# Cross-attention block on one core: scores before the next key, and a weight's upper parts moved from GpSimd to ScalarE in the opening

## The reference

```python
q  = layernorm(x) * q_norm_g + q_norm_b
kv = layernorm(ctx) * kv_norm_g + kv_norm_b
qp, kp, vp = q @ Wq.T + bq, kv @ Wk.T + bk, kv @ Wv.T + bv
scores = qh @ kh.T / sqrt(32) - spatial_scale[h] * dist(query_xy, token_xy) + spatial_offset[h]
scores = where(token_mask, scores, -inf)
x = x + softmax(scores) @ vh @ Wo.T + bo
x = x + gelu(layernorm(x) @ W1.T + b1) @ W2.T + b2
```

## Time and profile before

| | |
|---|---|
| median of 3 runs | 1207.32 us (1204.98 to 1208.12) |
| the profiled execution, own time | 1204.9 us |
| its span, the first to the last instruction | 1203.0 us |
| TensorE busy | 98% of the span |
| VectorE, ScalarE, GpSimd busy | 76%, 72%, 79% |
| mean granted TensorE clock | 0.997 |

### The profile page before, as it was taken

One profiled execution on the slowest core, in us unless ns is written; L12 is line 12 of the kernel. 1 busy time (PEld: TensorE's weight loads), 2 busy tenths in 40 slices (PEclk: granted clock), 3 DMA queues, 4 the chain that ended last, 5 costly groups with the idle time before them and its releaser, 6 DMA issues.

```text
span 1203.0 us, 27763 instructions
## 1 busy us (share of the span) xinstructions
PE 1181.3 (98%) x9632; PEld 806.3 (67%) x9632; DVE 912.4 (76%) x2482; ACT 863.4 (72%) x1964; POOL 953.5 (79%) x1198
## 2 busy tenths in 40 slices
PE   7899999999999999999999999999999999999999
PEld 4566666666676766667676666667666666766666
DVE  7987768787787978877797888778787877668322
ACT  5798787858677786867778786877778587757232
POOL 6889989788897988789798878889887887758321
PEclk9999999999999999999999999999999999999999
DMA  9776768989799898979989998889989797978553
GB/s 264 202 190 182 183 181 184 208 190 234 164 232 200 186 215 191 217 180 229 189 189 226 188 217 168 212 203 217 216 181 217 188 218 160 187 169 173 148 152 103
DMA packets 434524, 233.22 MB, mean 194 GB/s; under 512 B 349888, under 2 KB 374864, under 8 KB 434384
## 3 DMA queue, kind: packets, MB, share of 16 engines
q1 hardware_dynamic: 434384, 231.45, 83.7%
HBM read 109.66 MB, written 12.58 MB: 102 GB/s over the span
## 4 chain that ended last, share of the span: by engine, by line
PE 90%; ACT 4%; DVE 3%; DMA 1%; issue 1%; SPq 1%; DVEq 0%; ACTq 0%
PE ps_up L920 26%; PE ps_down L940 26%; PE ps_qk L821 13%; PE ps_vo L843 6%; PE ps_s L864 4%; PE ps_pv L846 3%; PE ps_pv L905 3%; PE ps_vo L846 3%; ACT soft L1111 1%; PE ps_down L968 1%; DVE soft L1441 1%; PE ps_down L876 1%; DMA w<-x_scratch 0%; ACT pT_whole L1124 0%; DMA w_stage<-in_w_qkv 0%
## 5 line engine op out<-in xcount | busy, mean ns | idle before, releaser
L920 PE MATMUL ps_up<-hT,w 128*128 128x256 f16 x3072 | 377.0, 273 | 0.0
L1111 ACT ACTIVATE soft<-soft,neg_max 128x256 f32<-128x256 f32 x512 | 255.6, 500 | 163.1 <-DVE neg_max L1441 161.8
L1441 DVE CUSTOM_DVE_ANT_0 soft<-ps_s,soft,factor 128x256 f32<-128x256 f32 x506 | 223.2, 477 | 188.8 <-PE ps_s L864 188.6
L940 PE MATMUL ps_down<-w,hid 128*128 128x512 f16 x1476 | 359.6, 378 | 0.8 <-ACT pT_whole L1124 0.6
L920 PEld LDWEIGHTS ps_up<-hT,w 128*128 128x128 f16 x3072 | 300.6, 98 | 85.9
L1683 POOL TENSOR_SCALAR p_nat<-soft,row_inv 128x256 f16<-128x256 f32 x448 | 265.9, 604 | 71.5 <-DVE row_inv L1454 67.8
L1692 POOL TENSOR_SCALAR soft<-dist,scale_neg,offset 128x512 f32<-128x512 f32 x256 | 271.4, 1060 | 17.3 <-DVE p_nat L1460 15.5
L1460 DVE SCALAR_TENSOR_TENSOR p_nat<-soft,row_inv,p_nat 128x256 f16<-128x256 f32 x448 | 268.5, 639 | 0.8 <-POOL p_nat L1683 0.8
L1164 ACT ACTIVATE u<-ps_up,bias,up_scale 128x256 f32<-128x256 f32 x256 | 142.5, 557 | 126.2 <-PE ps_up L920 123.4
L940 PEld LDWEIGHTS ps_down<-w,hid 128*128 128x128 f16 x1476 | 141.5, 97 | 127.0 <-issue 2.9
L1700 POOL TENSOR_SCALAR hid<-u,hid_scale 128x1024 f16<-128x1024 f32 x63 | 72.9, 1157 | 46.5 <-ACT u L1170 46.5
(11 more groups left out here) (180 smaller groups left out, 1549.2 us busy)
## 6 DMA issues: line engine op xcount, KB each, us to landing
w<-x_scratch SPq DMA_DIRECT2D x252, 256.0 KB, 3.1
stack<-qk_parts SPq DMA_DIRECT2D x256, 96.0 KB
raw<-in_ctx SPq DMA_DIRECT2D x32, 256.0 KB, 3.5
raw<-in_x SPq DMA_DIRECT2D x32, 256.0 KB, 4.2
c_stage<-in_w SPq DMA_DIRECT2D x16, 512.0 KB, 5.0
x<-in_x SPq DMA_DIRECT2D x32, 256.0 KB, 3.5
out<-x SPq DMA_DIRECT2D x31, 256.0 KB, 3.4
tok_rows<-in_tok_xy SPq DMA_DIRECT2D x16, 256.0 KB, 3.6
```

What stands on the lines that cost most here:

```text
L920: mm = e.matmul(ps_up[s % 2][:, 0:L], w_1_sb[:, wp, k, m * P:(m + 1) * P], hT[:, b % 2, :, xp * KT + k, :], start=(k, wp, xp) == (0, 0, 0) ...
L940: mm = e.matmul(ps_down[tt][:], left, w_2_sb[:, s % W2_RING, wp, :], start=first, stop=last)
L1111: e.activation(soft[:, ring, lc, :], soft[:, ring, lc, :], ACT.Exp, scale=-1.0, bias=neg_max[:, ring, lc:lc + 1], accum_out=row_sum[:, rin ...
L1441: e.tensor_tensor_reduce(soft[:, ring, lc, :], score_bank(i)[:, lc * T:(lc + 1) * T], soft[:, ring, lc, :], factor[:, 0:1], 3.0e38, ALU.ad ...
```

## The change

Seven edits:

- **Scores first.** The key of group 1 goes from slot -2 to -1, where it stands behind the scores of item 0. All that follows it moves one slot: its parts to slot 0, the query to 1, its parts to 2, the four copies to 3. The key of group 2 goes from slot 1 to 2, its parts to 3; its query stays. On ScalarE the upper parts of group 1 stand ahead of the slot's exponentials.
- **W_q's upper parts** (all four pieces of the rest) go from GpSimd to ScalarE, in slot -3 behind the square root of the distances.
- **W_q's lower parts:** the first two pieces go from slot -3 to slot 0, behind the maximum of item 0; the last two from slot 0 to 1.
- **W_k's lower parts:** one piece in slot -6 and three in -4, where there were two and two.
- **W_v's norm:** `total` goes from slot -3 to -1 behind the scores of item 0, `square_norm` from -2 to 0 behind the maximum of item 0, `norm_root` from -2 to -1. `gains` stays in slot 0.
- **No negation:** the coordinates stay as they are and the square takes scale=-1.0; `small_negate` is gone.
- The waits for the small inputs move with it.

```diff
-        TOTAL = (-30, -28, -3, 0, 2, 5, 9, 13, 17, 20, 23, 26)
-        NORM = (-27, -24, -2, 1, 3, 6, 10, 14, 18, 21, 24, 27)
+        TOTAL = (-30, -28, -1, 0, 2, 5, 9, 13, 17, 20, 23, 26)
+        NORM = (-27, -24, 0, 1, 3, 6, 10, 14, 18, 21, 24, 27)
...
-        def qk_at(slot, first):
-
-            yield from (G for G in due(slot, first, GROUP, N_HG) if G != 1)
-            if slot == first + GROUP + 1:
-                yield 1
+        QK_OPENING = {(1, 0): -1, (1, 1): 1, (2, 0): 2}
+
+        def qk_at(slot, which, by):
+
+            yield from (G for G in due(slot, QK_PROJ + 2 * which + by, GROUP, N_HG) if (G, which) not in QK_OPENING)
+            yield from (G for (G, of), at_slot in QK_OPENING.items() if (of, at_slot + by) == (which, slot))
...
                 if -1 <= slot < UP:
                     scores(slot + 1)
+                if slot == TOTAL_V:
+                    total(AT[SEC_V])
...
+            def query_hi_rest():
+                gate.wait_ge(s_gs, GAINED_Q)
+                for k in range(KT):
+                    e.activation(w_sec[SEC_Q][:, HI, k, P:D], w_stage[SEC_Q][:, k, P:D], ACT.Copy, scale=gain[:, SEC_Q, k:k + 1]).then_inc(s_rhi_q)
...
-                gate.wait_ge(s_cst, 1)
+                gate.wait_ge(s_small, 3 * DMA)
...
-                    e.activation(dst, tok_rows[:, c, :], ACT.Square, bias=q_neg[:, col:col + 1]).then_inc(s_sq)
+                    e.activation(dst, tok_rows[:, c, :], ACT.Square, scale=-1.0, bias=q_cols[:, col:col + 1]).then_inc(s_sq)
...
-                        if not 0 <= slot < UP:
+                        if G == 1 or not 0 <= slot < UP:
                             qk_hi(G, which)
...
+                if slot == -3:
+                    query_hi_rest()
...
-            def small_negate():
-                gate.wait_ge(s_small, 3 * DMA)
-                e.tensor_scalar(q_neg[:], q_neg[:], -1.0, None, ALU.mult).then_inc(s_cst)
...
                 for i in due(slot, 0, ITEM, N_ITEMS):
                     score_max(i)
+                if slot == NORM_V:
+                    square_norm(AT[SEC_V])
+                    weight_lo_rest(SEC_Q, range(2))
...
-                for sec, pieces, at_slot in ((SEC_K, range(2), -6), (SEC_K, range(2, KT), -4), (SEC_Q, range(2), -3), (SEC_Q, range(2, KT), 0)):
+                for sec, pieces, at_slot in ((SEC_K, range(1), -6), (SEC_K, range(1, KT), -4), (SEC_Q, range(2, KT), 1)):
                     if slot == at_slot:
                         weight_lo_rest(sec, pieces)
...
-            def weight_hi_rest(sec, pieces):
+            def key_hi_rest():
                 gate.wait_ge(s_gs, GAINED_Q)
                 gate.wait_ge(s_wpart[SEC_Q], KT)
-                for k in pieces:
-                    e.tensor_scalar(w_sec[sec][:, HI, k, P:D], w_stage[sec][:, k, P:D], gain[:, sec, k:k + 1], 1.0, ALU.mult, ALU.mult).then_inc(s_rhi)
+                for k in range(KT):
+                    e.tensor_scalar(w_sec[SEC_K][:, HI, k, P:D], w_stage[SEC_K][:, k, P:D], gain[:, SEC_K, k:k + 1], 1.0, ALU.mult, ALU.mult).then_inc(s_rhi_k)
...
+                if slot == NORM_V - 1:
+                    norm_root(AT[SEC_V])
...
-                for sec, pieces, at_slot in ((SEC_K, range(KT), -23), (SEC_Q, range(2), -21), (SEC_Q, range(2, KT), -2)):
-                    if slot == at_slot:
-                        weight_hi_rest(sec, pieces)
+                if slot == -23:
+                    key_hi_rest()
```

More of the change, by code:

```diff
@@ L265, in build_block @@
         s_wpart = {1: sem("s_wpart_k"), 0: sem("s_wpart_q")}
-        s_fhi, s_rhi, s_xhi0, s_head0 = sem("s_fhi"), sem("s_rhi"), sem("s_xhi0"), sem("s_head0")
+        s_rhi_k, s_rhi_q = sem("s_rhi_k"), sem("s_rhi_q")
+        s_fhi, s_xhi0, s_head0 = sem("s_fhi"), sem("s_xhi0"), sem("s_head0")
         s_gram, s_spread, s_top = sem("s_gram"), sem("s_spread"), sem("s_top")
@@ L675, in sync_program @@
                         mask_copy(ring)
-                for G in qk_at(slot, QK_PROJ + 4):
+                for G in qk_at(slot, 1, 2):
                     stack_copies(G)
@@ L995, in tensor_program @@
                 for which in range(2):
-                    for G in qk_at(slot, QK_PROJ + 2 * which):
+                    for G in qk_at(slot, which, 0):
                         for _ in range(STEPS):
@@ L999, in tensor_program @@
                 for w in range(N_W):
-                    if slot == TOTAL[w]:
+                    if slot == TOTAL[w] and w != AT[SEC_V]:
                         total(w)
@@ L1185, in scalar_program @@
                 for which in range(2):
-                    for G in qk_at(slot, QK_PROJ + 2 * which + 1):
-                        if not 0 <= slot < UP:
+                    for G in qk_at(slot, which, 1):
+                        if G == 1 or not 0 <= slot < UP:
                             qk_hi(G, which)
@@ L1196, in scalar_program @@
                 for which in range(2):
-                    for G in qk_at(slot, QK_PROJ + 2 * which + 1):
-                        if 0 <= slot < UP:
+                    for G in qk_at(slot, which, 1):
+                        if G != 1 and 0 <= slot < UP:
                             qk_hi(G, which)
@@ L1364, in weight_lo_rest @@
                 for k in pieces:
-                    gate.wait_ge(s_rhi, KT * AT[sec] + k + 1)
+                    gate.wait_ge(s_rhi_k if sec == SEC_K else s_rhi_q, k + 1)
                     sub = e.scalar_tensor_tensor(out=w_sec[sec][:, LO, k, P:D], in0=w_stage[sec][:, k, P:D], scalar=gain[:, sec, k:k + 1],
@@ L1537, in vector_program @@
                         diagonal(w)
-                    if slot == NORM[w]:
+                    if slot == NORM[w] and w != AT[SEC_V]:
                         square_norm(w)
@@ L1545, in vector_program @@
                     hidden_scales()
-                if slot == -26:
-                    small_negate()
                 if slot == -23:
@@ L1759, in gpsimd_program @@
                         x_hi(1, n)
-                for w in range(AT[SEC_V], N_W):
+                if slot == NORM_V - 1:
+                    norm_root(AT[SEC_V])
+                for w in range(AT[SEC_O], N_W):
                     if slot == NORM[w]:
                         norm_root(w)
-                for sec, pieces, at_slot in ((SEC_K, range(KT), -23), (SEC_Q, range(2), -21), (SEC_Q, range(2, KT), -2)):
-                    if slot == at_slot:
-                        weight_hi_rest(sec, pieces)
+                if slot == -23:
+                    key_hi_rest()
                 if slot == -22:
```

8 lines of the change are left out of this document (5 added, 3 removed).

## The result

| | before | after |
|---|---|---|
| median, taken on the same chip | 1204.59 us (1203.99 to 1208.12) | 1210.49 us (1208.85 to 1211.24) |
| the profiled execution, own time | 1204.9 | 1209.96 |
| its span | 1203.0 | 1208.2 |
| mean granted TensorE clock | 0.997 | 0.994 |

The ratio is 1.0041, with a 95% interval of 1.0029 to 1.0053: about 4.9 us slower. It is not the ratio of the two medians, which lie 5.9 us apart, because the executions of before fall into two groups some 3 us apart. The forecast was 2.1 us slower, read as "no change". The sign of the working was right, its size was less than half of what was measured.

The account below looks back on a forecast made before the run. It took VectorE to bound the opening and TensorE from item 6's scores on. Those scores run 2.1 us late, so 1207.32 + 2.1 = 1209.4 us, read as "no change"; range 1205.5 to 1212.0.

Parts of the forecast that it names:

- What bounds it: TensorE holds the chain from item 6's scores at 48.85 us; a shift there reaches the end nearly whole.
- The copies of group 1: Slot 3: copies take 4.1 us from issue, so item 4's scores start at 42.9 against 39.68, 3.2 late.
- Rival 1: Slot 3: item 4's scores don't wait for the copies; 1.3 us less, 1206.0; chance 0.13.
- The first maximum: Opening: item 0's scores at 26.0, so VectorE's maximum starts at 26.4 instead of 27.73, 1.3 us sooner.
- Rival 4: Opening: W_o's load holds item 0's copy, the maximum stays at 27.73, all behind 1.3 us later, 1210.7; chance 0.08.
- VectorE's list to the end of slot 2: From the first maximum to slot 2's end: 12.4 us against 10.9, ending at 38.8 against 38.65.
- rival 2: Behind the first maximum, W_q's four lower parts meet GpSimd: 2.2 us in all on top, 1211.6; chance 0.12.
- From M3 to item 6: From slot 2's end at 38.8 to item 6's scores at 50.9: 12.1 us, those scores 2.1 late.
- rival 3: Clock falls in the wait ahead of item 4's scores: 1211.1, chance 0.10; old fall vanishes instead: 1207.7, chance 0.05.
- W_q's upper parts on ScalarE: Slot -3: four pieces, about 2.2 us, fit ScalarE's idle time from 23.98; nothing lost.
- The scale in the square: Square of the coordinates: the scale rides in the same instruction, free, 0 us.
- the norm: W_v's norm, moved later: square_norm adds 0.2 us to VectorE's list, the later norm_root on GpSimd costs 0.

Follow-up runs that it names:

- e11: Kernel before with W_q's upper parts on ScalarE in slot -3 and ten filler matmuls in slots -4 and -3: 1203.82 us, ratio 0.9988.
- e2: Changed kernel with group 1 and group 2's key back in their old slots, W_q's last two lower parts in slot 0: 1207.96 us, ratio 1.0026.
- e8: Changed kernel with W_o's load issued behind group 0's copies instead of ahead of them: 1212.54 us, one execution.
- e4: Kernel before with only W_q's upper parts moved from GpSimd to ScalarE in slot -3: 1206.3 us, ratio 1.0001.
- e13: Kernel before with ten filler matmuls (6 in slot -4, 4 in slot -3) and nothing else: 1204.74 us, ratio 0.9996.
- e7: Like e2, with W_v's total, square_norm and root also back in slots -3 and -2: 1206.73 us, ratio 1.0009.
- e1: Changed kernel with 12 filler matmuls ahead of item 0's scores and 9 ahead of group 2's key: 1211.14 us, ratio 1.0044.
- e10: Changed kernel with filler matmuls ahead of the clock's fall, 8 in slot -4, 14 in -2, 9 in 2: 1210.15 us, ratio 1.0033.
- e12: Like e10, with W_1's total ahead of group 2's key and item 4's scores waiting for one copy: 1208.37 us, ratio 1.0024.

## Why the prediction was right or wrong

**What bounds it, and that a shift at item 6 reaches the end:** right. 5.3 at S6, 5.2 in the span.

**The copies of group 1:** right as a bound, and the core of the forecast. 4.15 us from the issue to item 4's scores, 4.1 predicted, though no row gave the 0.4 us in it for the receipt. In the kernels whose key and query of group 2 ran at full clock, M3 to S6 took 12.12 to 12.13 in the new slots, and 10.17 to 10.20 in the old ones (e11's 10.55 has that query at 2.77 us): 1.9 us, as the working had it (12.1 against 10.2). Undoing the slots (e2, with W_q's last two lower parts) gave 0.0015 back, 1.8 us with 1.9 on either side, and 2.2 at S6 in the profile. Rival 1, the gain carried, is refuted.

**The first maximum:** this is the largest term that failed, by 1.7 us. The step said that the copy for item 0 would be there at 26.0, "a little behind the load". "A little behind the load" held: it was read at 27.44, 0.3 us behind the load, as in seven other profiles. What failed is the load's own landing, which the step took over from before: 6.1 us behind its issue there, 25.7, but 7.3 in after, 27.1. Rival 4 had the mechanism, at a chance of 0.08, and e8 shows it. My bounds, 25.3 to 26.41, were too narrow: I had bounded the later end by the time of before, as if a copy issued sooner could not land later. Why the load lands later is open, but the runs narrow it. It took 5.6 to 6.3 us in before, e4, e11 and e13, and 7.2 to 8.3 in the nine profiles with the rest of the change, e7 among them (7.7), which has the slots and the norm of before. So it is none of slots, norm and W_q's upper parts by itself; W_q's first lower parts, W_k's split and the negation with its waits are left, and were not tried. The DMA share in 24 to 31 us doesn't tell the two sets apart: 1.02 in after, but 0.87 in before and in e1, whose load took 7.4.

**VectorE's list to the end of slot 2:** 12.78 against 12.4, and that this is close is luck: two errors nearly cancel. VectorE's busy time from M0 to M3 grew by 1.06 us (10.44 to 11.50) and not by 1.5, mainly as the two parts behind the first maximum took 1.14 us together where 1.49 had stood in before's list; its idle time grew by 0.8, which I had at nothing. W_q's four took 0.606 to 0.609 each, so rival 2, that they meet GpSimd, did not come true (the line's instructions in after, ns least/median/most):

```profile
L1376 DVE SCALAR_TENSOR_TENSOR w_q<-w_stage,gain,w_q x4: 606/607/609, 29.0 to 34.7; 128x384 f16<-128x384 f32 x4
```

The rule of the Trainium skill behind it ("SBUF — State Buffer", section "Who interferes with whom") was hardly put to the test: beside either pair GpSimd made the root of a norm, one number for each partition (29.19 and 34.38, 0.85 us), and its bias tiles began at 30.04 and 35.23, when the pairs were all but done. What I left out is what stands between item 0's and item 1's scores now. I costed VectorE's list and ScalarE's, and not TensorE's. With the key (2.72 at half clock) moved behind the first scores and the gram (1.26) behind it, VectorE waited 1.10 us for the gram. The wait is the half clock's: in e10 the key and the gram ran at full clock, VectorE had no wait there, and M1 came 3.3 us behind M0; in after 4.5, before 2.8.

**From M3 to item 6:** 13.27 against 12.1, short by 1.2. At full clock the 12.1 holds (12.12 in e10), so this is the price of the half clock in slot 3, and it came on a way that I had not listed: the key of group 2 took 2.54 us instead of 1.48, W_1's total stands behind it, VectorE waits 2.05 us for that total, and the key's lower parts come so late that TensorE waits 0.95 for them ahead of the query. The 8.0 us that I gave TensorE from item 4's scores to item 6's held, with these 0.95 on top. TensorE's idle stretch of over 2 us came too, but ahead of that key, which waits 2.46 for the query's lower parts, and only 0.57 of it ahead of item 4's scores. That way is also a second bound at full clock, as e12 shows, which the working did not have: with the copies in time the shift would have been no smaller.

**The clock, rival 3:** it came, and not only where I had put it. I looked for one fall ahead of item 4's scores; there was one there (0.57 in 41 to 45 us) and an earlier one, while TensorE waited for item 0's copy (0.51 in 24 to 31). The Trainium skill, "TensorE: Matmul & The Clock Gate", section "HAM oscillation — how this bites in real kernels", describes just this, matmuls that run slow behind a wait for a DMA; the trace agrees with it by the key's 2.72 us against 1.47. I gave the fall 0.10, by one stretch of the steady part, when the opening has long waits of its own. What it is worth here is not fully shown, since fillers moved it rather than ended it. The rows bound it: the two keys lost 1.25 and 1.07 us, 2.3 in all, and e10, with both keys at full clock and the fall on a query between them, was 0.8 sooner at S6.

**The other parts.** W_q's upper parts on ScalarE: 0, as costed (e4, 1.0001). The scale in the square is free as said: the squares took 0.50 us each before and after. Undoing the slots and the norm together (e7) took the ratio from 1.0041 to 1.0009, 3.9 us with 1.9 on either side. How that splits, 1.8 for the slots (e2) and 2.0 for the norm by the ratios, 2.2 and 0.1 by S6 in the profiles, is not shown, nor what the two lower parts behind the first maximum, W_k's split and the negation cost, since e7 is not clear of before (0.9998 to 1.0019). I had costed the norm at 0.2 on VectorE and 0 on GpSimd and had not asked which TensorE instruction waits for it: in the order of e2 it is W_o's gram, by 0.91 us; in the full change the key stands in that gap.

So the measured 4.9 us against the forecast's 2.1 are three terms at once (1.7, 0.4 and 1.2, together 3.2 at S6 by the profile), and they come from one habit: each engine's list, and the load, was costed by itself, at the durations of before. The forecast of the median itself, 1209.4, lies only 1.1 us under the 1210.49 measured, and that is luck: it set out from 1207.32, the median of three executions, where six gave 1204.59.

## What to carry to other kernels

When work is moved behind a wait so that the waiter starts sooner, ask first what that wait is for: here it was a transfer, it did not come sooner, and the moved key now stands ahead of the next reader. Look in the same queue for what was issued ahead of a small urgent copy, and leave some 4 us between the first of four such copies and their reader. To learn what a half clock costs, compare a kernel with the same kernel at full clock: e4 beside before made a slow key look free, and e4 beside e11 gave 1.2 us.
